# Q and K projected with the head as innermost column index, each block of a stacked operand moved by one 128-row DMA from the sync engine

## What is computed

```python
Q, K, V = x @ W_Q.T, x @ W_K.T, x @ W_V.T          # 16 heads of 32 columns
attn = einsum('bhqd,bhkd->bhqk', Q, K) / sqrt(32)   # causal
x = layernorm(x + (softmax(attn) @ V) @ W_O.T)
logits = x @ router_w.T + router_b                  # 8 experts
x = layernorm(x + expert[argmax](x) * max(softmax(logits)))
```

## Time and profile before

| | |
|---|---|
| runs | 2947.26, 2947.55, 2957.64 us |
| span of the profiled execution, first to last instruction | 2947.9 us |
| its own time, with what lies around the span | not given apart from the span |
| TensorE matmul busy | 2664.0 us, 90% |
| VectorE / ScalarE / GpSimd busy | 53% / 36% / 22% |
| mean granted TensorE clock, as a share of full | 0.968 |
| passes of attention | about 80 to 2552 us |
| experts | about 2580 to 2948 us |

### The profile page before, as it was taken

The page is one execution under the profiler, slowest core; times in us unless marked ns, Lnnn a source line. Parts: engine busy times, 40 slices in busy tenths (PEclk is TensorE's granted clock), DMA queues, the critical chain, the costliest instruction groups (busy, mean ns, idle before and its releaser), DMA issues. The chain is left out here.

```text
span 2947.9 us, 51268 instructions
## 1 busy us (share of the span) xinstructions
PE 2664.0 (90%) x16384; PEld 1627.8 (55%) x16385; DVE 1563.5 (53%) x2843; ACT 1065.4 (36%) x2153; POOL 660.7 (22%) x1022
## 2 busy tenths in 40 slices
PE   3999989998999999998999899989999999438886
PEld 2654665457554755475546654565447554436665
DVE  2566446645564456535663466445644564365554
ACT  2245314541445134522453145414541345132332
POOL 2111221113121311122112211131213110235544
PEclk9999999999999999999999999999999999669999
DMA  8422142314331433124221422152314320163332
GB/s 284 115 73 98 39 142 70 90 58 127 90 101 48 118 102 97 50 79 129 74 93 51 139 71 80 58 144 73 101 51 122 87 80 8 43 208 119 121 123 82
DMA packets 131006, 282.95 MB, mean 96 GB/s; under 512 B 33026, under 2 KB 42242, under 8 KB 128452
## 3 DMA queue, kind: packets, MB, share of 16 engines
q1 hardware_dynamic: 100920, 208.62, 23.7%
q0 software_dynamic: 28304, 70.64, 7.8%
q10 hardware_dynamic: 1536, 0.53, 0.1%
HBM read 133.04 MB, written 47.53 MB: 61 GB/s over the span
## 5 line engine op out<-in xcount | busy, mean ns | idle before, releaser
L638 ACT ACTIVATE probs<-score 128x512 f32<-128x512 f32 (+3 forms) x1536 | 690.2, 489 | 812.3 <-PE score L944 511.3
L695 DVE TENSOR_REDUCE tile_max<-maxp 128x1 f32<-128x512 f32 (+3 forms) x1072 | 679.7, 659 | 513.2 <-PE maxp L929 347.6
L940 PE MATMUL score<-q_stack,k_stack 97*128 97x512 f32 (+2 forms) x1536 | 548.5, 410 | 17.6 <-ACT probs L638 16.3
L880 PE MATMUL proj<-xt,w_qk 128*128 128x512 f32 x1536 | 458.8, 413 | 61.5 <-DMA w_qk<-w_qk_parts 49.8
L924 PE MATMUL maxp<-k_stack,q_stack 96*128 96x512 f32 (+2 forms) x1360 | 466.5, 397 | 16.2 <-DVE tile_max L695 12.5
L924 PEld LDWEIGHTS maxp<-k_stack,q_stack 96*128 96x128 f32 x1360 | 240.5, 193 | 312.3 <-issue 225.7
L940 PEld LDWEIGHTS score<-q_stack,k_stack 97*128 97x128 f32 x1536 | 290.3, 194 | 195.0 <-ACT probs L638 178.6
L880 PEld LDWEIGHTS proj<-xt,w_qk 128*128 128x128 f32 x1536 | 280.9, 193 | 118.5 <-DMA w_qk<-w_qk_parts 49.5
L962 PE MATMUL y_ps<-probs,v 128*32 128x512 f32 (+3 forms) x3072 | 327.5, 498 | 8.8 <-DVE rows L719 7.8
L962 PE MATMUL den_ps<-probs,ones_f 128*32 128x512 f32 (+3 forms) x3072 | 326.5, 497 | 0.0
L377 POOL DMA_DIRECT2D q_stack<-parts x256 | 126.6, 503 | 545.3 <-DVE parts L682 543.3
(11 more groups left out here) (138 smaller groups left out, 2312.0 us busy)
## 6 DMA issues: line engine op xcount, KB each, us to landing
w_qk<-w_qk_parts SPq DMA_DIRECT2D x64, 512.0 KB, 3.7
q_stack<-w_vo_parts SPq DMA_DIRECT2D x16, 2048.0 KB, 8.0
q_stack<-parts SPq DMA_DIRECT2D x512, 64.0 KB
k_stack<-parts SPq DMA_DIRECT2D x512, 64.0 KB
got<-dispatched SPq DMA_DIRECT2D x75, 257.0 KB
xt_raw<-x_t SPq DMA_DIRECT2D x32, 512.0 KB, 4.4
q_stack<-parts POOLq DMA_DIRECT2D x256, 64.0 KB, 2.3
k_stack<-parts POOLq DMA_DIRECT2D x256, 64.0 KB, 2.3
```

Source lines behind the costliest of these rows:

```text
L638: nc.scalar.activation(probs[:, 4 * (n % 2) + h, c:BANK], score[h % 2][:, c:BANK], ACT.Exp, scale=SCALE).then_inc(exp_done.sem, 1)
L695: nc.vector.tensor_reduce(tile_max[:, j, heads[0]:heads[-1] + 1, qb], tiles, AX.X, ALU.max)\
L880: mm = nc.tensor.matmul(proj[bank][:, :], w_qk[:, o, ws, k, :], xt[:, xs, k, t * BANK:(t + 1) * BANK], start=c == 0, stop=c == 3 * KT - 1)
L940: mm = nc.tensor.matmul(score[h % 2][:, c0:BANK], k_st[u % SETS][0:3 * DH + 1, h, kb * P:(kb + 1) * P], q_st[u % SETS][0:3 * DH + 1, h, t ...
```

## The change

The columns of W_Q and W_K are permuted on the host, inside each unit of 128, from (head, feature) to (feature, head). Row n of a projected tile is then feature n // 4 of head n % 4. A block of the stack, 32 rows by 4 heads by 512 columns, now lists its 128 pieces of 2048 bytes in the order in which the 128 rows of `parts` stand, and one DMA of 256 KB moves it. A tile takes 3 DMAs in place of 12, all issued by the sync engine. GpSimd issues none of them and no longer waits for the tiles; the two semaphores of a token half become one.

```diff
-        SP_BLOCKS = 2
-        SP_GAIN, POOL_GAIN = 4 * SP_BLOCKS * 16, 4 * (3 - SP_BLOCKS) * 16
-        sp_in = [signal(f"sp_in{i}", UNITS * 2 * SP_GAIN, 2 * SP_GAIN, dma=True) for i in range(2)]
-        pool_in = [Signal(ctx, nc, f"pool_in{i}", UNITS * 2 * POOL_GAIN, 0, 2 * POOL_GAIN) for i in range(2)]
+        STACK_ROWS = 3
+        STACK_GAIN = STACK_ROWS * 16
+        stack_in = [signal(f"stack_in{i}", UNITS * 2 * STACK_GAIN, 2 * STACK_GAIN, dma=True) for i in range(2)]
...
         def stacked(eng, b, slot, tiles):
-            for s, gain in ((sp_in[slot], SP_GAIN), (pool_in[slot], POOL_GAIN)):
-                eng.wait_ge(s.sem, s.early(tiles * gain) if b is None else s.at(b, tiles * gain))
+            s, count = stack_in[slot], tiles * STACK_GAIN
+            eng.wait_ge(s.sem, s.early(count) if b is None else s.at(b, count))
...
-            for block_row in blocks:
-                part = ((HI, HI, LO), (HI, LO, HI))[o][block_row]
-                for h in range(4):
-                    eng.dma_start(dst[DH * block_row:DH * (block_row + 1), h, t * BANK:(t + 1) * BANK].bitcast(F32),
-                                  parts[DH * h:DH * (h + 1), t, part, :].bitcast(F32)).then_inc(done[t].sem, 16)
+            for block_row, part in enumerate(((HI, HI, LO), (HI, LO, HI))[o]):
+                sp.dma_start(dst[DH * block_row:DH * (block_row + 1), :, t * BANK:(t + 1) * BANK].bitcast(F32),
+                             parts[:, t, part, :].bitcast(F32)).then_inc(stack_in[t].sem, 16)
...
-            def send(b, u):
-                for o in (Q, K):
-                    for t in range(HALVES):
-                        send_tile(pool, b, u, o, t, range(SP_BLOCKS, 3), pool_in, held_pool)
-            send(None, 0)
...
-                wait_last_batch(pool, b, proj_full)
...
-                send(b, 1)
-                wait_job(pool, b, proj_full, ("v", 6))
...
-                wait_job(pool, b, proj_full, ("v", 7))
...
-                send(b, 2)
...
-                weighed(pool, b, GROUPS)
...
-                send(b, 3)
...
-                if not last:
-                    send(b, 0)
...
+    def heads_innermost(w):
+        return np.asarray(w).T.reshape(D, UNITS, 4, DH).transpose(0, 1, 3, 2).reshape(D, D)
...
-        "wq_t": np.asarray(inputs["L0_attn_W_Q"]).T,
-        "wk_t": np.asarray(inputs["L0_attn_W_K"]).T,
+        "wq_t": heads_innermost(inputs["L0_attn_W_Q"]),
+        "wk_t": heads_innermost(inputs["L0_attn_W_K"]),
```

More of the change, by code:

```diff
@@ L366, in attend, with send_tile @@
         block = ctx.enter_context(nc.Block())
-        def send_tile(eng, b, u, o, t, blocks, done, held):
-            wait_job(eng, b, proj_free, ("p", u, 2 * o + t))
+        def send_tile(sp, b, u, o, t):
+            wait_job(sp, b, proj_free, ("p", u, 2 * o + t))
             if b is not None:
-                hold(eng, held)
+                hold(sp, held_sp)
             dst = (q_st, k_st)[o][u % SETS]
-            for block_row in blocks:
-                part = ((HI, HI, LO), (HI, LO, HI))[o][block_row]
-                for h in range(4):
-                    eng.dma_start(dst[DH * block_row:DH * (block_row + 1), h, t * BANK:(t + 1) * BANK].bitcast(F32),
-                                  parts[DH * h:DH * (h + 1), t, part, :].bitcast(F32)).then_inc(done[t].sem, 16)
+            for block_row, part in enumerate(((HI, HI, LO), (HI, LO, HI))[o]):
+                sp.dma_start(dst[DH * block_row:DH * (block_row + 1), :, t * BANK:(t + 1) * BANK].bitcast(F32),
+                             parts[:, t, part, :].bitcast(F32)).then_inc(stack_in[t].sem, 16)
         @block.sync
@@ L398, in send @@
                     for t in range(HALVES):
-                        send_tile(sp, b, u, o, t, range(SP_BLOCKS), sp_in, held_sp)
+                        send_tile(sp, b, u, o, t)
                     if not (u == UNITS - 1 and isinstance(b, int)):
@@ L506, in _ @@
             nc.gpsimd.memset(small[:, :, :], 0.0).then_inc(setup_done, 1)
-            def send(b, u):
-                for o in (Q, K):
-                    for t in range(HALVES):
-                        send_tile(pool, b, u, o, t, range(SP_BLOCKS, 3), pool_in, held_pool)
-            send(None, 0)
-            def one_pass(b, last):
-                wait_last_batch(pool, b, proj_full)
-                hold(pool, held_pool)
-                send(b, 1)
-                wait_job(pool, b, proj_full, ("v", 6))
-                hold(pool, held_pool)
-                wait_job(pool, b, proj_full, ("v", 7))
-                hold(pool, held_pool)
-                send(b, 2)
-                hold(pool, held_pool)
-                weighed(pool, b, GROUPS)
-                hold(pool, held_pool)
-                send(b, 3)
+            def one_pass(b, last):
                 for k in range(0 if last else KT):
```

## The result

The changed kernel took 3008.02 us (median of 4 runs, 3003.38 to 3016.64) beside 2952.60 us for the kernel before (median of 4 runs): 1.0193 times as long, with a 95% interval of 1.0170 to 1.0216. I had forecast 2946.5 and a range up to 2967. The change makes the kernel slower by 1.9%, and the forecast was wrong in sign and size. The profiled execution took 3003.38 us, with a span of 3001.6; the span before was 2947.9, so 53.7 us have to be found.

What follows compares the result with a forecast made beforehand. TensorE's matmuls, 90% of the span, bound the kernel, so DMA edits pay only where it waits, in openings. 2947.9 - 1.0 = 2946.9 us profiled, given as 2946.5 because the runs' median is 0.35 below the span; range 2909 to 2967.

Steps and rivals of the forecast that it cites:

- A tile lands sooner: Unit 0's stacks in the openings: a tile's last block lands after 3.9 us, not 6.7; credited 1 us, last pass.
- No wait in rows 3 is for those.: Weight loads and next-sequence rows behind tiles on sync's queue start up to 6 us earlier; no listed wait; credit 0.
- reading F: Made after measuring, not forecast: at a loop's jump, instruction fetches share the 16 DMA engines and stand behind stack blocks.
- What is late next is VectorE … whatever the stacks do: Openings: VectorE starts subtracting at 1016.69 regardless, so the fifth tile of maxima can't start before 1018.04.
- GpSimd and issue cost: GpSimd loses 512 sends, 254 us nobody waits for; sync issues 384 DMAs for 1024, 0.59 us each; credit 0.
- The third block: Its move from GpSimd's queue to sync's puts it amid the scatter in openings: 0, between -38 and +43 us.
- C: Rival: the burst of sends worsens the openings' scatter window, 19 us, so 2967, up to 2990; chance 0.19.
- B: Rival: fewer DMAs and signals end the openings' congestion, 38 us, so 2909; half the effect gives 2928; chance 0.33.
- D: Rival: the 128-row DMA is not cheap, 1.81 us an issue, 6.6 to land; 21 us, so 2968; chance 0.05.
- the first stall: In an opening, 0.39 us before the second job, where TensorE waits for unit 0's stacks; the forecast had it removed.
- I am wrong altogether if the time moves in the stretches of units: Stretches of units: TensorE busy 220.6 of 225.0 us at clock 0.99, so nothing there was expected to move.

Runs made afterwards that it cites:

- one block in flight: The changed kernel, but sync issues each 256 KB DMA only after the one before has landed: 3355.47 us, 1.1358 of the kernel before.
- spread blocks: The changed kernel with block r on rows r, r + 3, r + 6 and so on: 2952.69 us, 0.9997; with passes written out too, 2906.40 us, 0.9842.

## Why the prediction was wrong

*"A tile lands sooner" is the step that failed.* I took 2.7 us to land from the residual rows, a DMA of 128 rows from DRAM onto 128 partitions, and called a stack block the same thing. It isn't: the destination is 32 neighbouring partitions. A block takes 6.8 us to land with others before it, 3.9 alone (one block in flight), and 2.05 us of all DMA engines. "2 x 0.59 + 2.7 = 3.9" for a tile should have been 3 x 2.05 plus about 2, some 8 us, and 14 for K's pair (14.2 measured, from 1031.59 to 1045.8, against some 13.4 before), not "about 6 us earlier" but later. The number of rows was matched, the side that they were written to was not.

*"No wait in rows 3 is for those."* I let sync's queue decide who gets late, and priced DMA engines at nothing because they had been at 0.3 to 0.5. At 40% in the mean and 0.96 in bursts, they delay whatever else goes through them: by reading F the instructions at the loop's return (8.3 to 8.5 us in six passes), the negated maxima (23.2 us of waits), the weights (7.6 for 3.7). The first could not be seen before, since nothing waited for it for more than 1 us.

*"What is late next is VectorE … whatever the stacks do"* held only while the loop's return was free. In the earlier trace rows it came 3.42 us late by itself; now it has been idle for 10.51 us, for ScalarE's copy of a product that TensorE could not start.

*GpSimd and issue cost.* Busy time 408.3 (forecast 409) and 0.60 us an issue (0.59) were right. The credit of 0 for GpSimd missed the 6 us behind the last score: after the last scatter it used to take 12.95 us to reach the experts' part, now 7.65. The kernel with small DMAs all from sync has it too (7.99); why is open.

```profile
2633.51 0.14 POOL L1194 IOTA lane<- 128x8 f32 x1 [7.65 <-POOLq L149]
```

*The third block* at 0 between -38 and +43: the openings gained 23.0 us, but not by the move. The gap let the scatter pass first. Two slips of the sum are small: no row has the 0.63 us for an issue (the median is 0.591), and C's 19 us are added to 2947.9, not to 2946.5.

*The rivals.* B's gain didn't come: with a quarter of the DMAs and signals, pass 8 still takes 38.4 us. That is no clean test of B's mechanism, because the slow blocks keep the DMA engines at 0.89 there. With as few DMAs and spread blocks, both kernels unrolled, the seven openings beside a scatter took 33.6 to 34.6 us where the kernel before took 35.7 to 38.2, near the 34.5 that B named. How much of this is their number and how much their speed isn't shown. C named more load in the scatter's window; its place was wrong, since scatter and sends no longer met in six passes. D named the right mechanism, a 128-row DMA that isn't cheap because of how its rows fall onto 32 partitions, and got 0.05. Its price, 21 us, counted only the first stall; and I had made it hang on dear issues, while the issues stayed at 0.6 and the transfer was dear. The range left it out with C's tail. "I am wrong altogether if the time moves in the stretches of units": 14 us of it did, in unit 0, some 6 more in units 1 to 3, and 60.6 in closings, which I hadn't named at all.

The rule of the Trainium skill that I weighed under B (DMA: Bandwidth & Descriptors, Rules for kernel authors), that transfers under 64 KB are mostly overhead, pulled the wrong way: four of 64 KB in 2.3 us each, beside each other, became one of 256 KB in 6.8. The port rule of the Trainium skill (SBUF — State Buffer, Door 1: The DMA port swizzle) would have given, as an estimate, 1.2 us for a block (256 KB at 218 GB/s). That makes 3 x 1.2 plus about 2, some 5.6 us, for a tile: too low for what was measured, and already above my 3.9.

## What to carry to other kernels

Before DMAs are merged, look at which partitions the merged one writes, and compare with a row that writes the same ones: here 128 rows onto 32 neighbours ran at 128 GB/s the same rows onto every second partition at 383, and onto every third of 96, which took the whole loss away, at 234. One slice is the difference. Price a DMA not only by who waits for it but by how long it keeps the DMA engines, since everything else stands behind it, by reading F the jump at a loop's end too. And where a wait reads "issue" at a loop's return, look at the DMA share there before looking for a late operand.

## What the runs showed that I had not expected

- A loop's return depends on DMA traffic: TensorE's gap was at most 0.8 us in the kernel before, 8.3 to 8.5 behind 256 KB blocks at 128 GB/s, 7.2 with one third of them on GpSimd's queue, 3.7 behind spread blocks, and absent without a backlog or without a jump. That the instruction packets are what waits is inferred from these five cases and from when the packets move, at the end of the backlog; when they were asked for is in no record.
- Writing the passes out gains 21 us (0.8%) for the kernel before, 30 for the changed one and 46 for the spread blocks. So the gain doesn't follow TensorE's gap alone (under 0.8, 8.3 to 8.5 and 3.7 us a return).
- The same overlap costs 6 us an opening where indirect writes meet stack sends in four comparisons, and nothing in two; whether chips differ or something else does isn't shown. A comparison at one level alone would have put the changed kernel at 1.9% or at 3.3%.
